# ScalarE's order in an attention step, and padding rows written ahead of the tokens, in an attention and mixture-of-experts layer

## The reference

```python
x = x + layernorm(attention(layernorm(x)))       # 16 heads of 64, causal softmax, then a norm with gamma, beta
x = x + layernorm(experts(layernorm(x)))

def attention(x):                                # per batch
    q, k, v = x @ Wq[h], x @ Wk[h], x @ Wv[h]    # h = 0..15, each 256 x 64
    attn = softmax(causal(q @ k.T / 8))
    y = x + concat_h(attn @ v) @ Wo
    return norm(y) * gamma + beta

def experts(xt):                                 # 4096 rows, 8 experts, each row goes to its best 2
    probs = softmax(xt @ router_w); top_p, top_i = top_k(probs, 2)
    for e in range(8):
        out += gate_e * (gelu(xt @ w1[e]) @ w2[e])    # 128 -> 512 -> 128
```

## Time and profile before

| what | value |
|---|---|
| three runs, median (lowest to highest) | 707.59 us (707.39 to 709.84) |
| the profiled execution | 707.34 us, of which the span of the core is 705.6 |
| TensorE matmul / weight load busy | 677.8 us (96%) / 576.4 us (82%) |
| ScalarE busy | 552.3 us (78%) |
| VectorE busy | 547.0 us (78%) |
| GpSimd busy | 281.6 us (40%) |
| granted TensorE clock | 0.996 of full |
| DMA | 34.89 MB, 49 GB/s over the span |

### The profile page before, as it was taken

How to read it: one execution, slowest core, us unless ns; L and a number is a source line. 1 busy time by engine, 2 the same in 40 slices (tenths; PEclk the granted TensorE clock), 3 DMA queues, 4 the chain that set the end, 5 groups by cost and what they waited for, 6 DMA issues and landing times.

```text
span 705.6 us, 18101 instructions
## 1 busy us (share of the span) xinstructions
PE 677.8 (96%) x5762; PEld 576.4 (82%) x5763; DVE 547.0 (78%) x2557; ACT 552.3 (78%) x1815; POOL 281.6 (40%) x424
## 2 busy tenths in 40 slices
PE   6999999999999999999999999999989999999994
PEld 5788878888878888788888788888878999999951
DVE  5677798989899898989898888888897774444326
ACT  5888888889898888888898988888885664555515
POOL 3012234343434353432323231423213777755545
PEclk9999999999999999999999999999999999999998
DMA  7900000000000000000000000000020243322155
GB/s 170 280 9 9 9 9 25 16 25 9 25 9 25 8 26 14 19 25 17 25 8 24 10 24 9 24 13 14 22 66 27 70 118 113 104 76 76 51 196 181
DMA packets 40537, 34.89 MB, mean 49 GB/s; under 512 B 10528, under 2 KB 36128, under 8 KB 40448
## 3 DMA queue, kind: packets, MB, share of 16 engines
q1 hardware_dynamic: 34816, 23.81, 12.5%
q0 software_dynamic: 4544, 9.45, 3.8%
q10 hardware_dynamic: 1088, 0.54, 0.3%
HBM read 20.22 MB, written 13.56 MB: 48 GB/s over the span
## 4 chain that ended last, share of the span: by engine, by line
PE 70%; ACT 20%; DMA 3%; DVE 2%; issue 2%; POOL 1%; DVEq 0%; SPq 0%; POOLq 0%; ACTq 0%
PE PT1O L446 13%; PE SC L434 9%; PE M L704 9%; PE M L411 6%; ACT qk L1308 5%; ACT pT L1328 5%; ACT prob L1319 5%; PE M L413 4%; PE M L412 4%; PE SC L437 4%; PE A L457 4%; ACT pT L1325 3%; PE PT1O L465 3%; PE SC L411 3%; PE SC L412 2%; PE SC L413 2%
## 5 line engine op out<-in xcount | busy, mean ns | idle before, releaser
L808 DVE CUSTOM_DVE_ANT_0 SC<-SC,mask 128x128 f32<-128x128 f32 (+1 forms) x512 | 166.0, 385 | 3.8 <-PE SC L437 3.3
L1319 ACT ACTIVATE prob<-SC,nmax 128x256 f32<-128x256 f32 x256 | 135.6, 530 | 0.0
L1308 ACT ACTIVATE qk<-M 128x512 f32<-128x512 f32 x127 | 77.6, 611 | 54.7 <-PE M L413 54.7
L446 PEld LDWEIGHTS PT1O<-pT,v_sb 128*64 128x64 f32 x1024 | 63.4, 136 | 49.1 <-ACT pT L1328 30.5
L1313 ACT ACTIVATE prob<-SC,nmax 128x128 f32<-128x128 f32 x256 | 101.9, 420 | 1.5 <-DVE nmax L808 1.5
L446 PE MATMUL PT1O<-pT,v_sb 128*64 128x256 f32 (+1 forms) x1024 | 97.3, 332 | 5.2 <-ACT pT L1328 0.9
L820 DVE TENSOR_TENSOR prob<-prob,rden 128x512 f32<-128x512 f32 x128 | 89.7, 700 | 2.4
L1610 POOL DMA_INDIRECT expert_rows<-v_sb,got x74 | 73.2, 990 | 36.2 <-ACT v_sb L1470 17.5
L1599 POOL DMA_INDIRECT sent_rows<-rec,slot x64 | 64.8, 1013 | 51.3 <-DVE slot L1074 34.9
L434 PE MATMUL SC<-qk 64*128 64x256 f32 x512 | 83.5, 403 | 0.9 <-ACT prob L1319 0.6
L411 PE MATMUL M<-xt_hi,wqk_hi 128*128 128x256 f32 x254 | 83.2, 328 | 1.2 <-ACT v_sb L1332 0.8
(11 more groups left out here) (212 smaller groups left out, 1731.3 us busy)
## 6 DMA issues: line engine op xcount, KB each, us to landing
got<-sent_rows SPq DMA_DIRECT2D x39, 132.0 KB, 2.3
w_in<-expert_rows SPq DMA_DIRECT2D x8, 512.0 KB, 4.9
x_in<-L_attn_x SPq DMA_DIRECT2D x16, 128.0 KB, 2.1
w_in<-L_ffn_w SPq DMA_DIRECT2D x1, 2048.0 KB, 12.4
x_res<-L_attn_x SPq DMA_DIRECT2D x16, 128.0 KB, 2.1
w_sb<-L_ffn_w SPq DMA_DIRECT2D x8, 256.0 KB, 4.6
out<-prob SPq DMA_DIRECT2D x6, 256.0 KB, 2.1
sent_rows<-pad_rec SPq DMA_DIRECT2D x11, 132.0 KB, 4.8
```

The lines of the kernel that those rows point to most:

```text
L446: last = mm(PT1O[k * E:(k + 1) * E, cols], v_sb[:, t, h * E:(h + 1) * E], src[:, par, k, :], start=(t == 0), stop=(t == 1), skip_group_che ...
L808: last = v.tensor_tensor_reduce(SC[par][:, k, cols], SC[par][:, k, cols], m, -1.0, -MASKED, ALU.add, ALU.min, nmax[:, par, late, k:k + 1])
L1308: a.activation(qk[:, p % 2], src[:].rearrange("p (i s) -> p i s", i=2), ACT.Copy).then_inc(qk_sb, 1)
L1319: return a.activation(prob[:, slot, k, 1:3, :].rearrange("p n t -> p (n t)"), SC[par][:, k, LATE_Q], ACT.Exp, scale=-1.0, bias=nmax[:, par ...
```

## The change

Two things are changed. In each attention step ScalarE copies the transposes of pair p - 2 directly behind the copy of projection p + 2, and those of pair p - 1 directly behind the copy of projection p + 3; the two late exponentials of pair p, which stood between these, come behind both. The other part: the regions are filled with padding rows, 256 rows of each of the 8 regions by one DMA, 16 such DMAs during the attention, each ahead of the sends that may overwrite those rows. The eight stores of padding behind the last token, with the wait for them and the table `pad_row`, are gone. `send` waits for the fill (`fill_st`), GpSimd writes the second set of padding destinations one batch earlier, and a tile's rows lie in `got` with two neighbouring rows of DRAM in one partition ("(p t)") where the two halves of the tile were ("(t p)").

```diff
@@ shared constants
+        FILLED = [[], [], [0], [1, 2], [3, 4]] + [[b] for b in range(5, B)]
@@ batch(b) of SyncE
-                if isinstance(b, int) and b < 2:
+                if b < 2:
                     expert_weights(b)
+                for j in FILLED[b] if b < B else ():
+
+                    if j == 0:
+                        sp.wait_ge(sem("pad_ok"), 2)
+                    else:
+                        sp.wait_ge(sem("fill_st"), 16 * j)
+                    sp.dma_start(regions[:, j * ROWS:(j + 1) * ROWS, :].rearrange("e (p t) c -> p e (t c)", p=P),
+                                 pad_rec[:].rearrange("p e t c -> p e (t c)"))\
+                        .then_inc(sem("fill_st"), 16)
@@ load_tiles
-                    sp.dma_start(got[:, k], sent[bass.ds(rows[k], ROWS), :].rearrange("(t p) c -> p t c", p=P))\
+                    sp.dma_start(got[:, k], sent[bass.ds(rows[k], ROWS), :].rearrange("(p t) c -> p t c", p=P))\
                         .then_inc(got_ld[k], 16)
-
-            def pads():
-                sp.wait_ge(sem("pads_known"), 1)
-                sp.wait_ge(sem("pad_ok"), 2)
...
-            pads()
 
             sp.wait_ge(sem("sent_st"), 16 * K * NT)
-            sp.wait_ge(sem("pad_st"), 16 * NE)
@@ step of ScalarE
                 if more:
                     qk_copy(p + 2)
 
-                exps_early(p, 0)
+
                 if k == 0:
+                    exps_early(p, 0)
                     v_copy(1, 0, 0)
-                if k >= 1:
+                else:
                     pT_copies(p - 2)
-                exps_late(p, 0)
+                    exps_early(p, 0)
                 if more:
                     qk_copy(p + 3)
-                exps_late(p, 1)
                 if k >= 1:
                     pT_copies(p - 1)
+                exps_late(p, 0)
+                exps_late(p, 1)
                 exps_early(p, 1).then_inc(exp_done, 1)
@@ ScalarE, expert stage
-                    if n == 10:
-                        pads[:] = pad_rows()
-                        store_pads(NE // 2, 3 * NE // 4)
-                    if n == 11:
-                        store_pads(3 * NE // 4, NE)
@@ send of GpSimd
                 pool.wait_ge(sem("rec_ok"), r + 1)
+                pool.wait_ge(sem("fill_st"), 16 * (r + 1))
@@ batch(b) of GpSimd
-                if isinstance(b, int) and b == LAG + 1:
+                if b == 2:
                     pool.wait_ge(sem("spare_st"), 16 * UNUSED)
                     pad_ids(UNUSED)
```

More of the change, by code:

```diff
@@ L55, in sandwich_kernel @@
     back = nc.dram_tensor("expert_rows", (K * N + (NE + UNUSED) * ROWS, D), F32, kind="Internal").ap()
+    regions = sent[0:NE * CAP, :].rearrange("(e c) d -> e c d", e=NE)
     back_groups = back[0:K * N, :].rearrange("(g p r k) d -> g p r k d", g=NG, p=P, r=K)
@@ L171, in sandwich_kernel @@
         row_of = sb("row_of", [1, TILES], I32)
-        pad_row = sb("pad_row", [1, NE], I32)
         got = sb("got", [P, RING, 2, REC])
@@ L221, in sandwich_kernel @@
         LAG = 2
+        FILLED = [[], [], [0], [1, 2], [3, 4]] + [[b] for b in range(5, B)]
+        assert sum(FILLED, []) == list(range(N // ROWS))
         STEPS = NP // 2
@@ L308, in expert_weights @@
                         rows = sent[NE * CAP + k * ROWS:NE * CAP + (k + 1) * ROWS, :]
-                        sp.dma_start(rows.rearrange("(t p) c -> p t c", p=P), pad_rec[:, k])\
+                        sp.dma_start(rows.rearrange("(p t) c -> p t c", p=P), pad_rec[:, k])\
                             .then_inc(sem("spare_st"), 16)
@@ L336, in load_tiles @@
                         sp.wait_ge(back_st[k], 32 * it)
-                    sp.dma_start(got[:, k], sent[bass.ds(rows[k], ROWS), :].rearrange("(t p) c -> p t c", p=P))\
+                    sp.dma_start(got[:, k], sent[bass.ds(rows[k], ROWS), :].rearrange("(p t) c -> p t c", p=P))\
                         .then_inc(got_ld[k], 16)
-            def pads():
-                sp.wait_ge(sem("pads_known"), 1)
-                sp.wait_ge(sem("pad_ok"), 2)
-                rows = table_values(pad_row[0:1, :], NE * CAP - ROWS,
-                                    "an expert gets N rows at most, its region has CAP")
-                for e in range(NE // 2):
-                    sp.dma_start(sent[bass.ds(rows[e], ROWS), :].rearrange("(t p) c -> p t c", p=P), pad_rec[:, e])\
-                        .then_inc(sem("pad_st"), 16)
             over_batches(batch)
@@ L1066, in find_places @@
                 dve.drain()
-                if is_last(r):
-                    v.tensor_copy(pad_row[:], base[0:1, :]).then_inc(sem("pads_known"), 1)
                 v.tensor_reduce(slot_f[:], picked[:], AX_X, ALU.add)
@@ L1433, in between @@
                     records(B - 1)
-            pads = []
-            def pad_rows():
-                act.wait_ge(sem("pads_known"), 1)
-                act.wait_ge(sem("pad_ok"), 2)
-                return nc.values_load_multi_w_load_instructions(
-                    pad_row[0:1, :], engines=[mybir.EngineType.Activation], min_val=0, max_val=NE * CAP - ROWS,
-                    skip_runtime_bounds_check_because="an expert gets N rows at most, its region has CAP")[1]
-            def store_pads(first, end):
-                for e in range(first, end):
-                    nc.scalar.dma_start(sent[bass.ds(pads[e], ROWS), :].rearrange("(t p) c -> p t c", p=P), pad_rec[:, e])\
-                        .then_inc(sem("pad_st"), 16)
             def gelu(n, s, halves=range(2)):
```

## The result

The changed kernel takes 710.7 us (median of six runs, 710.62 to 711.26), the kernel before 707.65 us (six runs, 707.39 to 709.84): a ratio of 1.004, with an interval of 1.0027 to 1.0052. It is 0.4% slower, which is real, but inside what was set down as "within 0.5%". Forecast were 711.6 us. The profiled span is 708.8 us, where it was 705.6; the granted clock is 0.995 of full, where it was 0.996.

A forecast was written before the change was run, and what follows sets the result against it. The loop through the pT copies bounds the kernel, with the last exponential's loop only 0.15 us shorter. 5.5 - 1.4 + 0.5 + 0 + 0.9 - 1.5 = +4.0 us on 707.34 gives 711.3, for the median 711.6 us; range 704 to 717.

The forecast's parts named there:

- rival (a): Attention step: the last exponential replaces the pT copies as what TensorE waits for; 709.5 to 714.5 us, chance 0.58.
- The new wait of ScalarE: Attention step: ScalarE, ready at 1.58, waits 0.24 us for the second projection, whose copy can start at 1.82.
- The end of the exponentials takes the place of the pT copies: Attention step: the last scores' weights wait for ScalarE's exponentials, 46 or more times, some 30 us.
- +0.12 a third, fourth or first step, 46 times: Such attention steps (k = 2 to 62) grow from 7.89 to 8.01 us; +5.5 us in all.
- Second steps, -1.4: 15 second attention steps, bound by TensorE, gain 0.09 us each from earlier second transposes; bounds 0 and -4.
- VectorE's gate, +0.5: Second transposes: late normalisation costs 0.24 us in each of four late steps; bounds 0 and 7 us.
- The last step, +0.9: Last attention step: both late exponentials, 0.45 us each, delay ScalarE's chain behind it; bounds 0 and 1.5 us.
- The first step, 0: Attention step k = 0: a late exponential moved behind costs 0.45 us, the step after gains about as much.
- The fills, 0: 16 fills during the attention, 17.3 MB at 5.2 us each, are covered and cost 0.
- The padding stores gone, -1.5: End of the sends: without padding stores TensorE's 1.47 us idle for tile 16 goes; bounds 0 and -1.5 us.
- The rule of the Trainium skill: Product with V: all 30.5 us of TensorE's idle for the pT copies is gained, 675.6 us; chance one in a hundred.

The follow-up runs named there:

- late_ahead: Changed kernel with head 0's late exponential put back ahead of the second projection copy, both pairs' pT copies left where the change put them; 699.76 us, ratio 0.987.
- experiment 12: Changed kernel with every fill stored three times, one behind the other; 710.91 us, ratio 1.0038.
- second_pair_only: Changed kernel with ScalarE's old order, except that the pT copies of pair p - 1 stand ahead of the second late exponential; 702.95 us, ratio 0.9917.
- fills_old_order: Changed kernel with ScalarE's old order, keeping the fills and no padding stores at the end; 707.0 us, ratio 0.9978.
- last_step: late_ahead with both late exponentials ahead of the second pair of pT copies in the last attention step; 698.85 us, ratio 0.9868.
- order_only: Kernel before with ScalarE's new order alone, padding stores kept and no fills; 712.27 us, ratio 1.0058.
- both_again: late_ahead with both late exponentials ahead in the last attention step and the stores of tiles 8 and 9 ahead of the last sends; 700.19 us, ratio 0.9895.
- two_stores_ahead: late_ahead with only the stores of tiles 8 and 9 moved ahead of the last sends; 701.11 us, ratio 0.9899.

## Why the prediction was right, and where its sizes were off

The measured 710.7 us lies in the stated range and near the forecast 711.6, and the mechanism is the forecast one, rival (a). Of the three outcomes the prediction had slower by more than 0.5% as the likeliest (0.49); the one that came, within 0.5%, had 0.37.

**The new wait of ScalarE: right.** The second copy was put at 1.82 and starts at 1.81; 0.24 was the wait, some 0.23 is measured. late_ahead shows that it is the cause: filling it, with the pT copies left where the change put them, takes the time from 710.7 to 699.8.

**The end of the exponentials takes the place of the pT copies: right.** 46 waits of the last scores' weights were forecast and 46 are there. But they are 15.5 us, and with those of the matmuls 21.2, where some 30 were forecast, and 23 us (12.7 and 10.6) are left ahead of the product with V, which were to be "nearly gone". There the prediction had the product start at 3.3, as soon as pT0 ends. It starts at 3.50. V's projection stands ahead of it on TensorE, and its last matmul starts at 325.49, 0.32 before; in the first step k = 36 it is 0.33 from that matmul (309.10) to the product's weights (309.43), with no wait for ScalarE listed, and in late_ahead 0.32. So TensorE's own list has become the gate there, by these rows; no run moved it. This size does not touch the sum, for the exponentials are later still.

**+0.12 a third, fourth or first step, 46 times: mis-sized.** A third step grew by 0.07 and a first by 0.05. The 45 such steps from k = 2 to 61 grew by 3.2 us in all, of which some 0.6 is VectorE's gate (below); the 2.6 left stand against the 5.5 that were put. The prediction let everything behind the second pT copy slide by 0.27, to 6.10. The last sum's read starts at 5.78 (5.53 before), 0.25 later, and its row is 0.26 long where it was 0.30, so it ends 0.21 later, at 6.04. The rest of the working holds: 6.04 + 0.05 + 1.87 = 7.96. One term stood on other rows than it said: the 1.86 from the scores' weights to the next copy holds for third and fourth steps, while the first step of the earlier trace rows takes 2.06 for it.

**Second steps, -1.4: mis-sized.** They gave 0.2. In batches 1 and 2 they are 0.31 and 0.19 shorter, and in the later ones 0.08, near the 0.09 that was put; in batches 3 to 8 the normalisation ends at 1.85, past the threshold of 1.62, and they are 8.64 long (one 8.74), 0.12 more than before. The normalisation moved by 0.14 to 0.16 in the other steps, as was worked out (1.45 to 1.59, 1.71 to 1.86), but by 0.28 in these (1.57 to 1.85). The trace has the other 0.10: ahead of it VectorE adds to `base`, and this row takes 0.37 us where it took 0.27, in each of these six batches but one, where it takes 0.46. From batch 9 on it takes 0.17 in both kernels. The last section says what stands beside it.

**VectorE's gate, +0.5: right.** The step that the earlier trace rows show (k = 23) has its normalisation at 1.86, where 1.85 was put, and takes 8.21 us, 0.31 more than before. The gate can be read off TensorE in the kernel after:

```profile
201.29 0.20 PEld L467 LDWEIGHTS PT1O<-ident,prob 128*128 128x128 f32 x2 [0.34 <-DVE prob L824]
```

Four late ones were counted, and four first, third or fourth steps have the normalisation past 1.62: k = 20, 23 and 60, which lose 0.14, 0.25 and 0.17, and k = 62 (2.02), which is in the last stretch. The count left out the second steps, where six are late.

**The last step, +0.9: the number right, 0.96, in part by luck.** ScalarE's table load behind the attention starts 1.23 us later than before, counted from k = 62: 0.9 by the two late exponentials, as was said, and 0.32 since VectorE's normalisation, of which nothing was said, lets the last six transposes go at 10.78 and not at 10.46. Behind it 0.27 comes back, the pT copies having no wait left. **The first step, 0: right,** k = 2 starts at 28.83 in both. **The fills, 0: right,** and experiment 12 says so for three times as much.

**The padding stores gone, -1.5: the step that failed.** "Behind it TensorE's own work is next" was wrong. Behind the last send stand, on GpSimd, the stores of tiles 8 and 9, and the loads of tiles 16 and 17 wait for these stores too, since they overwrite the buffers that the stores read. That way round left only 0.6 to 0.8 us to gain: this kernel's end gained 0.61, the old order's 0.78, and late_ahead's, whose attention ends earlier, nothing. The load of tile 17 also took 3.40 us, where the earlier trace rows have 2.19 for tile 16. The load on the chain takes 3.19 to 3.75 us in the five kernels where such a store released it (after, fills_old_order, late_ahead, second_pair_only, last_step) and 2.01 to 2.38 in the four where the last send did (before, order_only, both_again, two_stores_ahead). Pieces of 1056 bytes are in both groups, so they are not the cause; what is was not tried. So the same reasoning that I used on the attention step, to look for the loop that comes second, was not used on the tail.

**The rule of the Trainium skill** (page "Perfetto Trace Analysis", section "Identifying Performance Opportunities") is to make the dependency finish sooner for which the most contended engine waits. What the prediction worked out from it, 675.6 us, fell. The wait that it points at went from 30.5 us to 12.7 and the kernel became 3 us slower. Such an edit is worth only the distance to the next loop, less what it delays there: second_pair_only, which shortens the same wait and delays nothing, gains 5.6 us, not 30.

The errors were of both signs: +4.6 put and +2.98 measured in the steps, -1.5 put and -0.6 at the end. That hid them, and this was luck: 711.6 forecast, 710.7 measured. The forecast's sum was better than its terms.

## What to carry to other kernels

When two engines wait for each other once per step, write down the second-longest way round before shortening the longest; the difference is all there is to gain until that one is shortened too, and the same goes for the tail of a kernel. In an in-order queue an instruction that is ready can be the cover of a wait that nobody sees: moving the exponential away exposed 0.23 us in each step, and putting one of the two back turned a loss of 0.4% into a gain of 1.2%. A transfer that was needed only a batch (some 30 us) later could be tripled here without a trace of it in the time.

## What the runs showed of the hardware

**Rows of ScalarE grow while it does not rest.** An ACTIVATE of the same shape has a longer row the longer the queue has run without a gap. In late_ahead the late exponentials of one step are 0.49, 0.53, 0.55 and 0.57 us long (starts at 316.80, 318.47, 319.60 and 320.39), in the changed kernel, with a gap of 0.23 ahead of the second copy, 0.49, 0.49, 0.51 and 0.52, with the spacings within 0.01 of each other. This is where 0.04 of the missing 0.06 of the +0.12 went. Whether the work does end later, or only the row does, can't be told from a row; that TensorE's load follows the row's end by 0.05 in both kernels (328.35 and 328.40, 321.05 and 321.10) speaks for the work.

**Two groups of runs.** The two kernels with padding stores at the end spread by 2.6 to 3.5 us from run to run (before 706.9 to 710.4, order_only 711.7 to 714.3); those with the fills mostly by 0.4 to 1.7, both_again's 3.4 being the exception. The spread goes with the clock: of the 33 runs of the kernel before in the first and the last group of experiments, 13 took 709.1 us or more, and 12 of these have a mean granted clock of 0.992 to 0.994; of the other 20, all under 708.8, 19 have 0.995 to 0.997. The slower runs of order_only (713.93, 714.29) and both_again (703.36) have 0.994 as well. A lower clock behind a wait at tile 16, as in two_stores_ahead, would fit; no such run of these kernels was profiled, so it is not shown.

**The clock at the edge.** An idle time of 2.71 us ahead of tile 16 was followed by the lower clock level, one of 2.54 at the same place in another kernel was not. Such a wait can have a second price, here 1.2 us on top of the first.

**VectorE held up by GpSimd's work.** The addition to `base` takes 0.17 us in batches where GpSimd has no weights to split. In batches 3 to 8 it falls beside a piece of that work, in the kernel before and then after:

```profile
147.85 0.27 DVE L1063 TENSOR_TENSOR base<-base,before 128x8 f32<-128x8 f32 x1
```
```profile
148.25 0.45 POOL L1621 TENSOR_TENSOR w_lo<-w_in,w_hi 128x128 fp32r<-128x128 f32 x1
148.36 0.37 DVE L1065 TENSOR_TENSOR base<-base,before 128x8 f32<-128x8 f32 x1
```

In before, after, fills_old_order and order_only, six rows each, it starts while a row of GpSimd runs and ends 0.02 to 0.04 us behind that row's end (here 148.73 behind 148.70), whatever length this gives it (0.26 to 0.46). In late_ahead GpSimd's row ends within 0.15 us of its start or begins after it, and it takes 0.17. So moving ScalarE's list by 0.17 us made VectorE meet another row of GpSimd and lose 0.10 more. No run moved GpSimd's work alone.
